# A twelve-layer decoder on one core: sign matrices prepared a stage earlier, the order of the opening and of the local heads, and biases as products of exact parts

## What is computed

```
x = x + f(_layernorm(x), weights of the layer)        # twelve times

# layer 0: Mamba
u, res = split(x @ W_in.T); u = silu(conv4(u) + b_conv)
y = (_s6(u, f...) + flip(_s6(flip(u), b...))) * 0.5 * silu(res); return y @ W_out.T
# _s6: delta = softplus(dt @ Wdt.T + bdt); h = exp(delta*A)*h + delta*B*u; y = C.h + u*D

# layers 3, 4, 5, 7 and 10: attention of several kinds, each ending in
return out @ Wo + bo                                   # layer 4 also v = ctx @ Wv.T + bv

# layer 6: local heads
q = q*cos + rotate_half(q)*sin; k = k*cos + rotate_half(k)*sin
scores = q @ k.T * scale + dist * slopes[head]         # masked to a causal band of 64
out = softmax(scores) @ v + softmax(q @ k[::64].T * scale) @ v[::64]
return out @ Wo

# layer 8: signs; k0, k1, k2 are bool and become +1 or -1
h = concatenate([x, -x]); h = relu(s0 * (h @ sign(k0))) * 2
h = relu(s1 * (h @ sign(k1))) * 2; return s2 * (h @ sign(k2))
```

## Time and profile before

| | us |
|---|---|
| runs | 4470.59, 4476.31, 4476.92 |
| median | 4476.31 |
| profiled execution, its own time | 4478.14 |
| its span | 4476.3 |

### The profile page before, as it was taken

One profiled execution on the slowest core, in us unless ns is written; L12 is line 12 of the kernel. 1 busy time (PEld: TensorE's weight loads), 2 busy tenths in 40 slices (PEclk: granted clock), 3 DMA queues, 4 the chain that ended last, 5 costly groups with the idle time before them and its releaser, 6 DMA issues.

```text
span 4476.3 us, 57633 instructions
## 1 busy us (share of the span) xinstructions
PE 3847.8 (86%) x20186; PEld 2643.3 (59%) x20186; DVE 3182.3 (71%) x7349; ACT 2163.2 (48%) x5232; POOL 1392.8 (31%) x963
## 2 busy tenths in 40 slices
PE   5778788768999989998999998788797979778997
PEld 2323233325666669986888885455565558336776
DVE  5989999995666667666888976566576754543768
ACT  5666667564544532222333348367576622432334
POOL 3989898981000000001222223553310000100004
PEclk8889998889999999999999998699998989878998
DMA  3434444442000000000000010000000010000000
GB/s 108 139 130 150 132 149 139 136 151 82 1 1 1 1 22 29 20 10 13 1 1 1 1 39 1 13 1 1 12 2 2 1 38 1 39 0 19 1 1 19
DMA packets 83426, 180.16 MB, mean 40 GB/s; under 512 B 9051, under 2 KB 14275, under 8 KB 80579
## 3 DMA queue, kind: packets, MB, share of 16 engines
q1 hardware_dynamic: 83139, 176.49, 11.8%
HBM read 173.84 MB, written 2.62 MB: 39 GB/s over the span
## 4 chain that ended last, share of the span: by engine, by line
PE 36%; DVE 12%; ACT 4%; issue 2%; POOL 1%; DMA 0%; DVEq 0%; ACTq 0%; POOLq 0%
PE PS L210 29%; PE PS L217 5%; DVE qg L2156 1%; DVE stat L287 1%; DVE p L3466 1%; PE PS L3187 1%; DVE hl L2387 1%; DVE qg L2151 1%; ACT p L2683 1%; ACT p L3479 1%; DVE XNr L324 1%; DVE W L2392 0%; DVE wc L3391 0%; DVE p L3631 0%; POOL far L3594 0%
## 5 line engine op out<-in xcount | busy, mean ns | idle before, releaser
L210 PE MATMUL PS<-db,cst 128*128 128x512 f32 x1024 | 544.8, 680 | 159.1 <-DVE db L1205 159.0
L1200 DVE TENSOR_TENSOR_SCAN db<-PS,db 128x512 f32<-128x512 f32 x512 | 591.3, 1204 | 46.0 <-ACT PS L1165 34.2
L210 PEld LDWEIGHTS PS<-db,cst 128*128 128x128 f32 x1024 | 208.0, 214 | 468.8 <-DVE db L1205 241.2
L217 PE MATMUL PS<-cst,p 128*128 128x128 f32 (+1 forms) x2880 | 394.3, 283 | 55.1 <-DVE pt L3151 23.5
L217 PEld LDWEIGHTS PS<-cst,p 128*128 128x128 f32 (+1 forms) x2880 | 335.6, 147 | 114.5 <-issue 36.7
L210 PE MATMUL PS<-xnT,W 128*128 128x256 f32 (+2 forms) x1072 | 338.9, 464 | 17.4 <-ACT pt L2709 7.5
L1146 POOL TENSOR_TENSOR db<-du,b 128x1024 f32<-128x1024 f32 x128 | 307.9, 2433 | 12.9 <-PE PS L210 11.4
L1146 POOL TENSOR_TENSOR db<-W,b 128x1024 f32<-128x1024 f32 x128 | 310.3, 2451 | 1.8 <-PE PS L210 1.4
L2105 ACT ACTIVATE p<-PS,sm 128x256 f32<-128x256 f32 x256 | 119.0, 470 | 376.8 <-DVE sm L2162 376.8
L210 PEld LDWEIGHTS PS<-xnT,W 128*128 128x128 f32 (+1 forms) x1072 | 214.4, 204 | 141.1 <-issue 95.0
L1972 POOL TENSOR_TENSOR rb<-rb,tb 128x512 f32<-128x512 f32 x32 | 41.1, 1285 | 798.8 <-DVE tb L1967 798.8
(11 more groups left out here) (445 smaller groups left out, 8615.0 us busy)
## 6 DMA issues: line engine op xcount, KB each, us to landing
b<-bc_rows SPq DMA_DIRECT2D x256, 256.0 KB, 3.6
c<-bc_rows SPq DMA_DIRECT2D x256, 256.0 KB, 3.7
W<-in_we SPq DMA_DIRECT2D x9, 1024.0 KB, 4.8
W<-in_w SPq DMA_DIRECT2D x1, 4224.0 KB, 13.1
W<-in_w SPq DMA_DIRECT2D x1, 4122.5 KB, 14.0
W<-in_w SPq DMA_DIRECT2D x1, 4100.0 KB, 12.2
W<-in_w SPq DMA_DIRECT2D x1, 2313.0 KB, 10.0
X<-in_x SPq DMA_DIRECT2D x4, 512.0 KB, 16.7
```

Of the source, the lines that this page charges most:

```text
L210: ins = T.matmul(out, l, r, start=first and i == 0, stop=last and i == len(pairs) - 1)
L217: ins = T.transpose(bank[0:m, c:c + r], s, ident[0:r, 0:r])
L1200: V.tensor_tensor_scan(db[:, f, r], self.ring.PS[:, self.BANKS[x % 3], r], db[:, f, r], 0.0, ALU.mult, ALU.add).then_inc(self.sc.sem, 1)
```

## The change

Four parts.

1. **Opening.** The columns of the first weights are put in another order, so that the first transfer (2212 columns, not 2048) holds all that the pass needs before its second group of products; who waited for the whole of the weights (`w_ready`) waits for this part (`win_ready`). The context's normalization and transposes leave `Start` and go into `FIRST` in pieces: `CTX` after `SILU`, `CTX + 1` after `LN` and, for DVE, `CTX + 2` after `MAX + 1`. Their buffers are now the tiles `gate` and `y`. The second half of DU on GpSimd comes after the first three `db` products. The ring of c tiles has four.
2. **Local heads.** GpSimd does rotation and keys of tiles 0 and 1 ahead of the 16 slopes.
3. **Signs.** SP loads the bytes during layer 7; GpSimd converts w0, w2 and the first 4096 columns of w1 there, in six operations over 2048 elements a partition, after its copies of batches 1 to 5. DVE in layer 8 splits x first and then converts the second half of w1.
4. **Biases** of layers 3, 4 (two), 5, 7 and 10. The bias row stands in partitions 0 and 32 of the weights. DVE rounds both into `bias_parts` (fp32r) and leaves in partition 32 the bias minus its rounded form; one product over 33 partitions with ones adds both parts. 88 products are concerned: 16 in each of layers 3 and 4, 8 more in layer 4 for v, and 16 in each of 5, 7 and 10.

```diff
+    def dve_bias(self, e):
+        V = e.eng
+        e.wait_ge(*self.w_ready)
+        V.tensor_copy(self.b_ones[0:33, :], self.E.K("one", 33))
+        V.tensor_copy(self.b_parts[0:33, :], self.b_in).then_inc(e.own, e.up())
+        e.wait_ge(e.own, e.ups)
+        V.tensor_tensor(self.b_parts[32:33, :], self.b_in[32:33, :], self.b_parts[32:33, :],
+                        ALU.subtract).then_inc(self.b_made.sem, 1)
+
+    def bias_product(self, e, i, rows=P):
+        e.wait_ge(*self.b_made(1))
+        return [(self.b_ones[0:33, 0:rows], self.b_parts[0:33, i * D:(i + 1) * D])]
+
     def pe_to_x(self, e, t, parts, bias=None):
         bank = self.ring.take(e, ("x", self.n, t), self.x(t + 1))
         if bias is not None:
-            parts = parts + [(self.E.ones[0:1, :], bias)]
+            parts = parts + self.bias_product(e, bias)
         mm(e.eng, bank[:, 0:D], parts).then_inc(self.wo.sem, 1)
...
-        self.c_ = [E.tile(f"c{i}", 512) for i in range(3)]
+        self.c_ = [E.tile(f"c{i}", 512) for i in range(4)]
...
+        self.prev.place(self.G, self.Y, other[:, 8192:8320])
...
+        self.todo[2].append((self.READY, 0, self.DU + 1))
...
-             CONV + 3, UA + 1, SILU, DT, DT + 1, DTA, ROWS, WDT, DLA, WDT + 1, DLA + 1, WDT + 2, DLA + 2, WDT + 3, DLA + 3,
-             ABS, EXP, LN, MAX, MAX + 1, DU, DU + 1)
+             CONV + 3, UA + 1, SILU, CTX, DT, DT + 1, DTA, ROWS, WDT, DLA, WDT + 1, DLA + 1, WDT + 2, DLA + 2, WDT + 3,
+             DLA + 3, ABS, EXP, LN, CTX + 1, MAX, MAX + 1, CTX + 2, DU)
...
     def sp_c(self, e, i):
         c, p, d, k, s = self.of(i)
-        e.wait_ge(*self.c_used(i - 3))
-        e.eng.dma_start(self.c_[i % 3], self.bc[k, 16 + s].partition_broadcast(P)).then_inc(self.cd_[i % 3].sem, 16)
+        e.wait_ge(*self.c_used(i - 4))
+        e.eng.dma_start(self.c_[i % 4], self.bc[k, 16 + s].partition_broadcast(P)).then_inc(self.cd_[i % 4].sem, 16)
...
+            if self.follow:
+                self.follow.pool_signs(e, b)
...
+        for t in range(2):
+            self.pool_rope(e, t)
+        for t in range(2):
+            self.pool_keys(e, t)
         for r in range(4):
-            for g in range(4):
...
+            self.pool_far(e, r)
...
+    def pool_signs(self, e, b):
+
+        G = e.eng
+        if b == 1:
+            e.wait_ge(*self.k0(1))
+            G.tensor_scalar(self.w0, self.raw0[:, 0, :], 2.0, None, ALU.mult)
+            G.tensor_scalar(self.w1[:, 2048:4096], self.raw0[:, 1, :], 2.0, None, ALU.mult).then_inc(e.own, e.up())
+        if b == 2:
+            e.wait_ge(e.own, e.ups)
+            G.tensor_tensor(self.w0, self.w0, self.w1[:, 2048:4096], ALU.subtract).then_inc(self.rp.sem, 1)
+        if b == 3:
+            e.wait_ge(*self.k2(1))
+            G.tensor_scalar(self.w2, self.raw2, 2.0, -1.0, ALU.mult, ALU.add).then_inc(self.rp.sem, 1)
+        if b in (4, 5):
+            e.wait_ge(*self.k1(1))
+            e.wait_ge(*self.rp(2))
+            c = slice(2048 * (b - 4), 2048 * (b - 3))
+            ins = G.tensor_scalar(self.w1[:, c], self.raw1[:, 0, c], 2.0, -1.0, ALU.mult, ALU.add)
+            if b == 5:
+                ins.then_inc(self.rp.sem, 1)
...
+        self.dve_split(e, 0)
         e.wait_ge(*self.ks(1))
         V.tensor_scalar(self.sc[:, 4:6], self.sc[:, 0:2], 2.0, None, ALU.mult).then_inc(self.rs.sem, 1)
-        for i in range(2):
-            e.wait_ge(*self.k1(i + 1))
-            V.tensor_scalar(self.w1[:, 4096 * i:4096 * i + 4096], self.raw, 2.0, -1.0, ALU.mult, ALU.add).then_inc(
-                self.r1.sem, 1)
-        self.dve_split(e, 0)
+        e.wait_ge(*self.k1(1))
+        V.tensor_scalar(self.w1[:, 4096:8192], self.raw1[:, 1, :], 2.0, -1.0, ALU.mult, ALU.add).then_inc(
+            self.r1.sem, 1)
```

More of the change, by code:

```diff
@@ L521, in __init__ @@
         self.first = 0 in LAYERS
-        self.raw, self.nrm = [a.rearrange("p (t d) -> p t d", t=8) for a in (E.W1[:, 0:2048], E.W1[:, 6144:8192])]
-        self.st = [E.tile(f"ctx_st{h}", 64) for h in range(2)]
+        self.place(E.W1[:, 0:2048], E.W1[:, 6144:8192], E.W1[:, 8192:8320])
         self.stats, self.sd, self.xn = [E.counted(x, 2 * context) for x in (
@@ L529, in __init__, with place @@
         E.ctx_ready = [self.ca(4), self.cd(4)] if context else []
+    def place(self, raw, nrm, st):
+        self.raw, self.nrm = [a.rearrange("p (t d) -> p t d", t=8) for a in (raw, nrm)]
+        self.st = [st[:, 64 * h:64 * h + 64] for h in range(2)]
     def x_done(self, t):
@@ L561, in dve, with dve_context, dve_stats @@
             self.nxt.dve(e, s, self.nxt.early)
-        if self.context:
-            self.dve_context(e)
-    def dve_context(self, e):
+        if self.context and not self.first:
+            self.dve_context(e, 0)
+            self.dve_context(e, 1)
+    def dve_context(self, e, norm):
+        if norm == 0:
+            self.dve_stats(e)
+        for i, (src, dst, k, h) in enumerate(self.banks):
+            if i % 2 and src == norm:
+                e.wait_ge(*self.tp(i + 1))
+                e.eng.tensor_copy(dst[:, k, 4 * h * S2:4 * (h + 1) * S2],
+                                  self.ring.of(("ctx", i))[:, 0:4 * S2]).then_inc(self.cd.sem, 1)
+        if norm == 0:
+            self.dve_apply(e)
+    def dve_stats(self, e):
         V = e.eng
@@ L595, in act, with act_context @@
             self.nxt.act(e, s, self.nxt.early)
-        if self.context:
-            self.act_context(e)
-    def act_context(self, e):
+        if self.context and not self.first:
+            self.act_context(e, 0)
+            self.act_context(e, 1)
+    def act_context(self, e, norm):
         C = e.eng
-        for h in range(2):
+        for i, (src, dst, k, h) in enumerate(self.banks):
+            if i % 2 == 0 and src == norm:
+                e.wait_ge(*self.tp(i + 1))
+                C.activation(dst[:, k, 4 * h * S2:4 * (h + 1) * S2], self.ring.of(("ctx", i))[:, 0:4 * S2],
+                             ACT.Copy).then_inc(self.ca.sem, 1)
+        for h in range(2) if norm == 0 else ():
             mv, bs, sd, rs = self.parts(h)
@@ L613, in pe, with pe_context @@
             self.nxt.pe(e, s, self.nxt.early)
-        if self.context:
-            self.pe_context(e)
-    def pe_context(self, e):
+        if self.context and not self.first:
+            self.pe_context(e, 0)
+            self.pe_context(e, 1)
+    def pe_context(self, e, norm):
         e.wait_ge(*self.c_in(1))
@@ L620, in pe_context @@
         for i, (src, dst, k, h) in enumerate(self.banks):
+            if src != norm:
+                continue
             if src:
@@ L1013, in act_piece @@
         delta = self.delta[d]
-        if self.UP <= j < self.UA:
+        if j >= self.CTX:
+            if j < self.CTX + 2 and self.prev.context:
+                self.prev.act_context(e, j - self.CTX)
+        elif self.UP <= j < self.UA:
             f = j - self.UP
@@ L1082, in dve_piece @@
         delta = self.delta[d]
-        if self.MAX <= j < self.ADD:
+        if j >= self.CTX:
+            if j != self.CTX + 1 and self.prev.context:
+                self.prev.dve_context(e, (j - self.CTX) // 2)
+        elif self.MAX <= j < self.ADD:
             r = j - self.MAX
```

193 lines of the change are left out of this document (100 added, 93 removed), and 2 rows, old and new, of the table SPEC.

## The result

The changed kernel took 4413.0 us in the median of four runs (4403.28 to 4421.57), the kernel before 4476.61; the ratio is 0.986, 95% interval 0.9835 to 0.9884. Forecast: 4419, 4392 to 4452. Its profiled execution (4403.28, span 4401.5) is the fastest of the four. Measured once more (e11), it took 4404.7 in the median of four, ratio 0.984 (0.9826 to 0.9855).

The account below looks back on a forecast made before the run. PE was taken to set the pace in the five bias stages, and PE's or DVE's last wait at the other changed places. Terms sum to -57.7 on 4478.14, 4420.4, so 4419 us for the median; range 4392 to 4452.

Parts of the forecast that it names:

- Opening: Start and Mamba: PE starts 9.9 us earlier; with the context's pieces, a removed wait and DVE stalls, -6.8 us.
- +1.0 for the transposes inside the pass: Opening: the context's 32 transposes find PE waiting, but an ACT copy hands on one of their banks: +1.0 us.
- The move of du: Opening, GpSimd's second half of du after three products: first scan's wait goes, -3.0 us; two DVE stalls come, +4.1.
- c ring: Mamba: a fourth c tile lets SP load two steps further ahead, -3 us, between 0 and -10.
- Local heads: Local heads: with rotation and keys ahead of the slopes, PE's transposes for the third rotation come 8.1 us earlier.
- Signs: Start of the sign layer: DVE splits x at once, so PE's first product comes 15.4 us earlier.
- GpSimd in layer 7: Layer 7: six GpSimd conversions of about 6.5 us each stall DVE by 10.0 us; +7 us reach the end.
- it calls itself wrong if stage 7 grows: Layer 7: a sign said to refute the forecast, namely that this stage gets longer; no size given.
- Biases: Five bias stages: one record instead of two saves 0.50 us on each of 88 biases, 44 of PE; -34.4 passed on.
- (a): Layer 7: GpSimd holds DVE longer, by slower byte conversion or a late batch 2 copy; +20, 4439 us; chance 0.14.
- (b): Bias stages: half the gain, since freed PE waits for DVE or ACT; 17 us, giving 4436; chance 0.13.
- (c): Whole kernel: more comes through, all 44 us of biases, -10 in the opening, c waits -7; about 4400; chance 0.09.

Follow-up runs that it names:

- e11: The changed kernel measured again, unchanged: 4404.7 us in the median of four.
- e8: The kernel before, unchanged, for a second trace: 4478.1 us.
- e4: Changed kernel with the opening as before (context in front of Mamba, 2048 columns first), but four c tiles: 4409.6 us.
- e5: Changed kernel with the second half of du on GpSimd in front of the first three db products again: first scan at 70.5, Mamba ends at 1031.3 us.
- e6: Changed kernel with three c tiles as before: 4411.9 us in one run.
- e7: Changed kernel with the 16 slopes in front of rotation and keys on GpSimd again: 4423.9 us in one run.
- e2: Changed kernel with the sign matrices loaded and converted in layer 8 as before: 4416.6 us.
- e1: Changed kernel with its 88 bias products back in float32, two records each, without the small DVE operations: 4449.0 us.
- e9: Changed kernel whose bias product takes one fp32r row, the rounded part only: 4408.1 us.
- e3: Changed kernel with GpSimd's multiplications by a factor written as multiply and add 0.0: 4396.6 us, ratio 0.9819.
- e10: Changed kernel whose bias product takes 33 rows in float32, two records, with the small DVE operations kept: 4446.8 us.
- e12: The kernel of e3 with a pause of 11 DVE buffer fills in front of everything: 4414.2 us.

## Why the prediction was right, and where it was not

The time lies in the range, 6 us under the forecast by the first median and 14 by the second. The waits were read rightly in the opening, the local heads and the signs; that the total fits is in part luck, since the price of a bias was too high and gains of the clock that nobody forecast made up for it. The steps:

- **Opening**, -6.8: at the scan -9.1 against the first trace of before, -5.5 against e8 and -2.9 against e4. The start of PE was right to 0.15 us, the two stalls cost 4.0 for 4.1, and the wait of 3.02 went. The +1.0 for the transposes inside the pass shows in no trace by itself: from PE's first product to DVE's delta chain it is 38.7 and 39.6 us in the changed kernel, 37.8 to 39.7 with the old order. What the step had not seen is that its 9.9 stood on one landing of the context: against e8 it is 7.5, against e4 5.6. The move of du, +1.1 by the prediction's own terms (-3.0 and +4.1), cost 1.7 in e5.
- **c ring**, -3: measured -3.5 to -4.9 against one trace (e6), inside its bounds.
- **Local heads**, -8.1: PE's transposes came 8.2 earlier, the layer shrank by 10. The difference goes with the granted clock, 0.93 to 0.96, and e7 takes both back.
- **Signs**, -15.4: the first product came 15.1 earlier, the layer shrank by 11.8, by 15.1 against the longer one of e8 and by 12.6 against e2. The failed assumption is that the products behind it would stay as they are: they are 0.0064 us further apart, 512 times.
- **GpSimd in layer 7**, +7: measured +5.5. The mechanism was right, the places were not. The price of 6.5 an operation was 5.36 or 1.90 by form. The normalizations of p named in the sum kept their 1.30; all that DVE lost is one small operation, held for 3.4 us by the subtraction, and the rest of the 5.5 goes with the lower clock (0.92 against 0.95 in e2). One test of the prediction contradicts its own sum: it calls itself wrong if stage 7 grows, but has +7 and -5.6 for it. The stage grew by 0.2. "Bytes are in no row" was worth a rival; bytes turned out not to be the point. The page's rule, GpSimd "roughly line-rate" on one input (the Trainium skill, GPSIMD Engine Reference, 4.1 Engine selection), fits the multiply-and-add form over 2048 bytes (1.90 us, 0.93 ns an element) and not multiplying alone (2.6 ns); over 512 float32 elements the form that fits still took 0.88 us, 1.7 ns each. The row of 1.635 us that decided against the rule was of multiplying alone.
- **Biases**, -34.4: e1 says -36 to -44, and yet the step failed. Its term "48 of those took 5.91 us, 0.12 each" is the price in a row of equal products; alone between float32 products it is 0.31. The 0.50 saved is 0.31, 88 times 27 and not 44. By the prediction's own test ("wrong if a bias record costs 0.3 us or more in its place") it was wrong here, and what filled the term up was the clock: some 10 us in the small attention, some 9 in layers 8 and 9. Two errors met. The talking heads show it the other way round: forecast -6, measured -1.0, at a clock of 0.99 before and 0.98 after; against e1, at the same 0.98, it is -2.9.
- **Nothing in layer 9**: 0 forecast, -9.0 measured. The same instructions stand there. The stretches where it goes, before and after:

```profile
3942.10:3962.70 20.60, 18.66 (x47) 9.64 (x45) 7.65 (x25) 6.80 (x10) 0.00 (x0) 0.71 0.00 1
3962.70:3989.00 26.30, 18.47 (x56) 9.48 (x57) 14.23 (x49) 8.31 (x12) 0.00 (x0) 0.82 0.00 0
```

```profile
3880.70:3896.30 15.60, 13.74 (x46) 7.01 (x44) 7.15 (x21) 6.51 (x10) 0.00 (x0) 1.00 0.00 0
3896.30:3920.10 23.80, 15.84 (x56) 8.52 (x56) 14.68 (x54) 8.52 (x13) 0.00 (x0) 0.90 0.00 1
```

The same work takes 46.9 us at 0.71 and 0.82 of the full clock, and 39.4 at 1.00 and 0.90. It is a mean of two levels, 2.4 and 1.2 GHz; before, part of the stretch ran at the lower.

Of the rivals, (a), longer stalls, did not come. (b), the biases at half, was right on the record (27 of 44) and wrong on the reason, and the clock hid it. (c), more of everything, is nearest to the e11 median of 4404.7, but by its number alone: it has all 44 of the biases, of which 27 are there.

**What stays open.** Layer 9 takes 237 us in the changed kernel and in e2, e4, e5, e6, e9 and e11, and 244 to 246 in e1, e3, e7, e10, e12 and before, with no instruction of it changed. Layer 8, where its products are the same, goes along (195.9 or 198.4). It is no chance of one execution, since the changed kernel and e11, and the kernel before and e8, repeat it; it is not the time at which the layer starts (e12), nor layer 8 alone (e2 had 208.5 in it and 236.6 behind). Each of the kernels that lose it differs in layers 3 to 7 from those that don't; but e2, with a shorter layer 7, and e9, with a longer small attention, differ there too and keep it. The two kinds part at the very start of layer 9: in all 14 traces the clock falls there, 1.4 to 1.9 us after the start of the layer where it is short and 3.9 to 4.7 us after it where it is long, well ahead of the stretches shown. Which feature of the work ahead decides was not settled.

## What to carry to other kernels

Price an instruction from a row in which it stands as it will stand: a run of 48 equal products says 0.12 us for something that costs 0.31 alone. Where PE's clock changes between two levels, cut both traces at fixed points of the work and compare piece by piece, the unchanged pieces first: here 9 of 75 us came from a layer that nobody touched, and 7.4 us of records were worth 17 to 19 us in the small attention, 5.0 us of them 0.7 in layer 5 (e10). Read the wait of the engine that sets the pace (34 us), not the largest wait in the list (90 us).

## What the runs showed of the hardware

- A GpSimd `TENSOR_SCALAR` with one operation costs 1.9 to 2.8 times the same with two, the second adding 0.0: 5.36 against 1.89 us for 2048 bytes to fp32r, 1.64 against 0.88 for 512 elements with a factor from SBUF, 1.01 against 0.46 for 320 with a constant.
- A DVE operation of 0.16 us on 8 elements waited 3.4 us for a GpSimd operation over two SBUF inputs; three of DVE's operations over 1024 elements took 2.0 us more each while GpSimd worked on two-input operations over 1024, and two of the three did not in e5, where GpSimd was idle at that time.
- A product over 1 row and one over 33 rows cost the same 0.31 us between float32 products, the float32 pair 0.62 or 0.63.
- Taking 24 short records out of a layer of 1024 moved its granted clock from 0.85 or 0.86 (e1, e10) to 0.90 (0.88 in e9), which was worth more (10 us) than the records (7.4).
- 508 gaps between equal products at full clock were 0.2334 us in the changed kernel and 0.2270 before and in e2, which places its tiles as before; the cause was not tried.
- The landing of one early transfer differed by 4.2 us between executions of the same order of transfers (11.5, 13.4 and 15.8).
